# Flamingo gated layer: eight small transfers per quad issued from ScalarE's queue instead of SyncE's

## The reference, cut to what matters

```
x   (8, 512, 1024), ctx (8, 512, 1024), mask all ones, 16 heads of 32 channels
q = Wq @ layernorm(x) + bq ; k = Wk @ ctx + bk ; v = Wv @ ctx + bv     # per batch, channels first
dot  = q^T k / sqrt(32), masked ; p = softmax(dot, over keys)
x    = x + tanh(g_xattn) * (p v)
y    = fp8(layernorm(x) * scale) / scale ; w = fp8(W2 * scale1) / scale1
out  = x + tanh(g_ffn) * (y @ w)
```

## Time and profile before

| | us |
|---|---|
| median of the runs | 2694.86 (2690.07 to 2695.24) |
| the profiled execution's own time | 2675.94 |
| its span, first to last instruction | 2674.1 |
| PE busy | 2539.9 (95%) |
| DVE / POOL / ACT busy | 1990.7 / 1651.7 / 1425.5 |
| granted TensorE clock, mean | 0.977 |
| share of the chain that ended last: PE / DMA / `den_c<-den` of it | 62% / 6% / 5% |

### The profile page before, as it was taken

One profiled execution on the slowest core, in us unless ns is written; L12 is line 12 of the kernel. 1 busy time (PEld: TensorE's weight loads), 2 busy tenths in 40 slices (PEclk: granted clock), 3 DMA queues, 4 the chain that ended last, 5 costly groups with the idle time before them and its releaser, 6 DMA issues.

```text
span 2674.1 us, 41111 instructions
## 1 busy us (share of the span) xinstructions
PE 2539.9 (95%) x13425; PEld 1401.9 (52%) x13425; DVE 1990.7 (74%) x3251; ACT 1425.5 (53%) x2638; POOL 1651.7 (62%) x1265
## 2 busy tenths in 40 slices
PE   5999999969999999999999999999999999999995
PEld 4888888854444444444444444444444444444441
DVE  5766666738777888788777777887888888878763
ACT  2333333314565666565656556666666666656663
POOL 1433333314776777677766777777777777767674
PEclk8999999987999999999999999999999999999998
DMA  6666666553333344444333333333333444444301
GB/s 207 245 238 237 239 238 238 211 154 58 74 82 82 91 96 91 86 98 95 87 83 86 82 82 82 82 82 82 90 83 90 96 92 95 93 87 90 84 29 40
DMA packets 208250, 306.12 MB, mean 114 GB/s; under 512 B 41241, under 2 KB 108889, under 8 KB 208065
## 3 DMA queue, kind: packets, MB, share of 16 engines
q1 hardware_dynamic: 195920, 265.80, 39.6%
q10 hardware_dynamic: 12144, 38.02, 4.0%
HBM read 200.09 MB, written 102.11 MB: 113 GB/s over the span
## 4 chain that ended last, share of the span: by engine, by line
PE 62%; DMA 6%; DVE 5%; issue 3%; POOL 1%; ACT 1%; SPq 0%; DVEq 0%; ACTq 0%; POOLq 0%
PE s_bank L694 18%; PE o_bank L720 17%; PE x_bank L707 15%; PE d_bank L731 7%; DMA den_c<-den 5%; PE x_bank L755 4%; DVE part_max L872 4%; PE x_bank L746 1%; POOL pair_sum L965 1%; PE x_bank L738 1%; DMA q_st<-qx_scr 0%; ACT den L812 0%; DVE y L103 0%; POOL y L974 0%; ACT probs L800 0%
## 5 line engine op out<-in xcount | busy, mean ns | idle before, releaser
L965 POOL TENSOR_TENSOR pair_sum<-probs 128x512 f32<-128x512 f32 x1024 | 1283.4, 1285 | 544.6 <-ACT probs L800 544.6
L872 DVE TENSOR_REDUCE part_max<-x_bank 128x1 f32<-128x512 f32 x2048 | 1279.4, 682 | 375.2 <-PE x_bank L707 368.2
L800 ACT ACTIVATE probs<-s_bank 128x512 f32<-128x512 f32 x2048 | 1071.5, 604 | 656.4 <-PE s_bank L694 650.4
L694 PE MATMUL s_bank<-q_st,k_st 100*128 100x512 f32 x2048 | 876.1, 430 | 4.6 <-ACT probs L800 4.6
L707 PE MATMUL x_bank<-k_st,q_st 98*128 98x512 f32 x2048 | 826.7, 407 | 55.1 <-DVE part_max L872 32.8
L694 PEld LDWEIGHTS s_bank<-q_st,k_st 100*128 100x128 f32 x2048 | 387.0, 189 | 513.2 <-issue 265.7
L720 PE MATMUL o_bank<-probs,v_t 128*32 128x512 f32 x4096 | 551.3, 611 | 0.0
L707 PEld LDWEIGHTS x_bank<-k_st,q_st 98*128 98x128 f32 x2048 | 392.9, 192 | 182.8 <-DVE part_max L872 62.8
L731 PE MATMUL d_bank<-pair_sum,ones 128*32 128x512 f32 x2048 | 269.4, 598 | 2.7 <-POOL pair_sum L965 2.7
L322 POOL TENSOR_TENSOR stage_lo<-stage,stage_hi 128x512 fp32r<-128x512 f32 x128 | 186.5, 1480 | 120.8 <-ACT stage_hi L392 120.2
L392 ACT ACTIVATE stage_hi<-stage 128x512 fp32r<-128x512 f32 x128 | 79.8, 632 | 190.4 <-DVE stage L476 142.8
(11 more groups left out here) (99 smaller groups left out, 2102.4 us busy)
## 6 DMA issues: line engine op xcount, KB each, us to landing
k_st<-k_scr SPq DMA_DIRECT2D x96, 512.0 KB
q_st<-q_scr SPq DMA_DIRECT2D x192, 256.0 KB
c_raw<-in_ctx_dram ACTq DMA_DIRECT2D x32, 512.0 KB, 7.0
x_raw<-in_x_dram ACTq DMA_DIRECT2D x32, 512.0 KB, 6.2
k_scr<-stage_hi SPq DMA_DIRECT2D x64, 256.0 KB, 2.4
k_scr<-stage_lo SPq DMA_DIRECT2D x64, 256.0 KB, 2.6
v_scr<-stage SPq DMA_DIRECT2D x64, 256.0 KB, 2.7
q_scr<-stage_hi SPq DMA_DIRECT2D x64, 256.0 KB, 2.1
```

Of the source, the lines that this page charges most:

```text
L694: nc.tensor.matmul(s_bank_of(n, k)[:, :], k_st[p][0:KS, h, j * P:(j + 1) * P], q_st[p][0:KS, th, h, :], start=True, stop=True).then_inc(sc ...
L800: nc.scalar.activation(probs[:, c % PR, h, :], s_bank_of(n, k)[:, :], ACT.Exp).then_inc(exp_done, 1)
L872: nc.vector.tensor_reduce(part_max[:, th, sh, at:at + 1], x_bank_of("tile", k)[:, :], AX, ALU.max).then_inc(max_done, 2)
L965: nc.gpsimd.tensor_tensor(pair_sum[:, r % 2, h], probs[:, a, h], probs[:, a + 1, h], ALU.add).then_inc(pair_done, 1)
```

## The change

Eight transfers of a period change engine: `move_den`, `move_inv`, `spread_inv` and `set_max`, each for both halves of a quad, leave SP's stream and are written into ScalarE's, at fixed slots between the exponentials. On SP stay `stack`, `load_res`, `load_v`, `load_tm` and `store`. The semaphore `stacked`, which counted the loads of q and k over all quads, is split by the parity of the quad, because SP can now run ahead with the loads of the second quad. Sizes, data and conditions of the transfers are unchanged. The functions themselves move word for word, with `act` for `sp`.

```
-            stacked = [sem(f"stacked{i}", at) for i in range(TH)]
+            stacked = [[sem(f"stacked{i}{th}", at) for th in range(TH)] for i in range(2)]
...
-                            pe.wait_ge(stacked[th], 16 * STACK_DMAS[th] * (m + 1))
+                            pe.wait_ge(stacked[p][th], STACK_DMAS[th] * loads_of_parity(m, p))
...
+                    def move_den(m, th):
+                        act.wait_ge(den_copied, 2 * m + th + 1)
+                        act.dma_start(den_c[:, :], den[0:P:D, :]).then_inc(den_moved, 16)
...
+                            if k == 13 and real(n - 1):
+                                move_den(n - 1, 1)
+                            if k == 24 and real(n - 1):
+                                move_inv(n - 1, 1)
+                            if k == 24 and real(n):
+                                set_max(n, 1, p)
+                            if k == 29 and real(n - 1):
+                                spread_inv(n - 1, 1)
+                            if k == 45 and real(n):
+                                move_den(n, 0)
+                            if k == 57 and real(n):
+                                move_inv(n, 0)
+                            if k == 62 and real(n):
+                                spread_inv(n, 0)
...
+                            if k == 56 and real(n + 1):
+                                set_max(n + 1, 0, 1 - p)
...
-                        if real(n - 1):
-                            move_den(n - 1, 1)
-                            move_inv(n - 1, 1)
-                        if real(n):
-                            set_max(n, 1, p)
-                        if real(n - 1):
-                            spread_inv(n - 1, 1)
```

More of the change, by code:

```diff
@@ L825, in copy_y8, with move_inv, spread_inv, set_max @@
                                              x_bank_of("turn_y8", 27)[:, :].bitcast(BF16), ACT.Copy).then_inc(y8_copied, 1)
+                    def move_den(m, th):
+                        act.wait_ge(den_copied, 2 * m + th + 1)
+                        act.dma_start(den_c[:, :], den[0:P:D, :]).then_inc(den_moved, 16)
+                    def move_inv(m, th):
+                        act.wait_ge(inv_done, 2 * (2 * m + th + 1))
+                        act.dma_start(inv_scr[th].rearrange("h (u v) -> (h u) v", u=D), inv_c[:, :]).then_inc(inv_moved, 16)
+                    def spread_inv(m, th):
+                        act.wait_ge(inv_moved, 16 * (2 * m + th + 1))
+                        if counted(NORM_STEPS * (m - 1) + 1):
+                            act.wait_ge(norm_done, NORM_STEPS * (m - 1) + 1)
+                        act.dma_start(inv_b[:, th, :], inv_scr[th].unsqueeze(1).broadcast_to((QH, D, HALF))).then_inc(inv_spread, 16)
+                    def set_max(m, th, p):
+                        act.wait_ge(max_copied, 2 * m + th + 1)
+                        act.dma_start(q_st[p][KX:KS, th, :, :].bitcast(F32), max_rows[:, :].bitcast(F32)).then_inc(max_set, 16)
                     def scale_rstd(m):
@@ L1012, in stack @@
                         for at, part in ((0, 0), (D, 1), (2 * D, 0)):
-                            sp.dma_start(k_st[p][at:at + D, :, :].bitcast(F32), k_part[part]).then_inc(stacked[0], 16)
-                        sp.dma_start(k_st[p][96:KS, :, :].bitcast(F32), kx_q[:, bass.ds(m, 1), :].broadcast_to((4, QH, S))).then_inc(stacked[0], 16)
+                            sp.dma_start(k_st[p][at:at + D, :, :].bitcast(F32), k_part[part]).then_inc(stacked[p][0], 16)
+                        sp.dma_start(k_st[p][96:KS, :, :].bitcast(F32), kx_q[:, bass.ds(m, 1), :].broadcast_to((4, QH, S))).then_inc(stacked[p][0], 16)
                         for th in range(TH):
                             for at, part in ((0, 0), (D, 0), (2 * D, 1)):
-                                sp.dma_start(q_st[p][at:at + D, th, :, :].bitcast(F32), q_part[part][:, th]).then_inc(stacked[th], 16)
+                                sp.dma_start(q_st[p][at:at + D, th, :, :].bitcast(F32), q_part[part][:, th]).then_inc(stacked[p][th], 16)
                             row = qx_q[:, bass.ds(m, 1), th * HALF:(th + 1) * HALF]
-                            sp.dma_start(q_st[p][96:98, th, :, :].bitcast(F32), row.broadcast_to((2, QH, HALF))).then_inc(stacked[th], 16)
+                            sp.dma_start(q_st[p][96:98, th, :, :].bitcast(F32), row.broadcast_to((2, QH, HALF))).then_inc(stacked[p][th], 16)
                     def load_v(m, p):
@@ L1024, in load_v @@
                         sp.dma_start(v_t[p][:, :, :], v_scr[bass.ds(m, 1), :, :].rearrange("o (j s) d -> s (o j) d", s=P)).then_inc(v_loaded[p], 16)
[L1026 to L1040, removed]
                     def load_tm(m):
@@ L1069, in period @@
                             load_v(n + 1, 1 - p)
-                        if real(n - 1):
-                            move_den(n - 1, 1)
-                            move_inv(n - 1, 1)
-                        if real(n):
-                            set_max(n, 1, p)
-                        if real(n - 1):
-                            spread_inv(n - 1, 1)
                         if real(n):
                             load_tm(n)
-                        if real(n):
-                            move_den(n, 0)
                         if real(n - 2):
                             store(n - 2, p)
[L1083 to L1088, removed]
                     run(period)
```

3 lines of the change are left out of this document (removed).

## The result

The kernel after has a median of 2842.20 us (2842.01 to 2842.94, 4 runs) against 2693.74 of the kernel before beside it (2690.07 to 2695.24, 4 runs): ratio 1.0568, 95% interval 1.0539 to 1.0596. The forecast was 2650 and the range ended at 2696. The profiled execution has a span of 2840.3 us against 2674.1, and a mean granted clock of 0.945 against 0.977.

What follows compares the result with a forecast made beforehand. TensorE, 95% busy, was taken to stop mainly for the denominators' transfer queued behind loads; -39 + 3 + 1 = -35 us on 2675.94 gave 2641, or 2660 with a constant offset; forecast the middle, 2650, range 2632 to 2696.

Steps and rivals of the forecast that it cites:

- Part 4: SP's stream: its loads keep their start and contention, its remaining waits stand before `load_tm` and `store` alone; cost nothing.
- Part 3: Waits moved into ScalarE's stream: `spread_inv` issued later, landing just before `weigh` needs it; +1 us, bounds 0 and +9.
- Part 2: Cost to ScalarE of issuing eight transfers per period, delaying exponentials, chiefly in slot 13: +3 us, bounds 0 and +46.
- rival C: Slower: ScalarE's slot 13 issue takes 2.8 us each period, TensorE pays and its clock falls; 2725 us, chance 0.14.
- the price of 41 us: TensorE's stops for `den_c` and the half clock behind them, in the profiled execution; the most their removal can give.
- Part 1: `move_den` of th = 1 on ScalarE's queue passes the loads, landing 4.3 us after issue: -39 us.
- the bound of 11 us: What remains if all the short TensorE stops of 0.38 us stay, over 29 periods.
- residue of 2: Allowance, in us, for periods in which line 900 misses its boundary with GpSimd's pair sum by a little.
- Rival B: Denominators land as late as before, descriptors of both queues being handled behind the loads; 2697 us, chance 0.13.
- The +3: Us charged for ScalarE's `den_c` issue in slot 13 possibly being as slow as SP's there.
- the slack of 0.3 us: Margin expected between the landing of the spread inverse, near 1539.7, and GpSimd's `weigh` at 1540.00; 5.3 us before.
- the two readings of the 18.9 us: Runs' median above the profiled execution: constant offset, giving 2660 us, or more long stops, giving near 2641.

Runs made afterwards that it cites:

- e1: Kernel after, with `spread_inv` of th = 0 issued by SP again, ahead of the next loads: 2655.65 us, 0.9881 of the kernel before.
- e3: Kernel after, with each spread of the inverse cut into four transfers, one per head: 2657.51 us, 0.9888 of the kernel before.
- e4: Kernel after, with `spread_inv` of th = 0 moved from slot 62 to slot 25 of the next period: 2658.28 us, 0.9879 of the kernel before.
- e2: Kernel before, all transfers on SP, with the spread of th = 0 held until right before the loads: 2838.97 us, ratio 1.0563.
- e9: Kernel after, with 256 of the 512 columns in the spread of th = 0: 2694.66 us, 1.0039 of the kernel before.
- e10: Kernel after, with 64 of the 512 columns in the spread of th = 0: 2665.80 us, 0.9934 of the kernel before.
- e6: Kernel before, with SP issuing `move_den` of th = 1 ahead of `load_res` and `load_v`: 2629.63 us, ratio 0.9791.
- e5: Kernel before, with only `move_den` of th = 1 moved to ScalarE, in slot 13: 2647.53 us, ratio 0.9861.
- the probe: Extra 128 x 16 element transfer on ScalarE's queue in slot 6, added to the kernel after with the th = 0 spread in slot 25: 2655.16 us.
- e7: Kernel after with the th = 0 spread in slot 25, SP holding `load_res` and `load_v` until th = 1 denominators landed: 2631.18 us, 0.98 of the kernel before.

## Why the prediction was wrong, point by point

**Part 4, and the start of `spread_inv` in Part 3: the step that failed.** Part 4 said of SP's loads that "neither their start nor their contention changes". The start was right (they still begin with the last scores), the contention was not: it is the spread of half th = 0 that comes to meet them. Part 2 has the same gap: it took all slots but 13 to have no load in flight, from a stretch near slot 29, and slot 62 lies 0.4 us before the loads. Part 3 followed `spread_inv` of th = 1 from 1529.91 to slot 29 and never that of th = 0, from 4.3 us before the loads to 0.4 us before them. One transfer of 256 KB on four engines delays the loads by 5.8 us, since a load has landed only when its slowest engine has (the 17 late updates of 104). The margin of slot 19, which the prediction did not read, was 16.85 - 15.8 = 1.1 us. Cost: 142.9 us of stops and most of 57.2 us at a lower clock. e1, e3 and e4 take that away in three ways, e2 puts it into the kernel before, and e9 and e10 scale it. No rival had this mechanism; rival C, slower as well, named ScalarE's issue, which didn't slow.

**What bounds the kernel, and the price of 41 us: nearly right.** Removing the wait altogether is worth 46 us of the span (2674.1 to 2628.0 in e6), 52 between medians. The value is 5 to 11 above the ceiling I gave; a period of the kernel without any stop is 61.4 us, where I took 62.10 - 0.38 = 61.72.

**Part 1: its value nearly right by luck, its mechanism wrong.** The move alone (e5) brought 34 us, and -39 + 3 were forecast. But the estimate that each short packet waits for one load packet, and so a landing after 4.3 us, failed: 9.0 us in e5, 8.9 in e1, 9.2 in e4, 12.3 in the kernel after itself, 10.0 for the probe. A landing that still takes 10 us was the prediction's own sign of being wrong. By the medians the other queue wins only 0.7 to 1.0 us over the 9.9 of the kernel before; that is enough to tip the long stops into short ones, and the short ones stay, the bound of 11 us that Part 1 named and not its residue of 2. The rest of the gain, 18 us between e5 and e6 on one chip, needs the order: e6 and e7 issue the denominators before the last megabyte of loads. Rival B was the better description of the transfer and the poorer one of the time. The prediction counted 8 packets for each engine; the transfer runs on four, so it has 32. With that the same estimate would have given 32 x 0.3 + 1.9 = 11.5 us; but the probe, on 16 engines, took 10.0 as well, so the count of engines does not explain the landing either.

**Part 2: right.** ScalarE's issue of `den_c` over the whole program, against SP's in the earlier trace rows:

```profile
L829 ACTq DMA_DIRECT2D den_c<-den x64: 549/554/605, 669.2 to 2805.4; - x64
```

It never slows, though the DMA engines are as full then (share 1.08 from 1516 to 1520), so the slow issues of SP in the earlier trace rows belong to SP's queue and not to the full DMA engines. The +3 should have been 0.

**Part 3, the rest: within its bound.** `weigh` waits for the spread 13.9 us in all, 11.4 of them in the tail, where the kernel before waits 10.6. The other 2.5 us are nine short waits: the slack of 0.3 us was used up in nine periods. What they cost TensorE no run separates.

**The sum and the offset: not shown.** Which of the two readings of the 18.9 us is right no run decides; the kernel before had medians from 2681.7 to 2694.9 us in its groups of runs, so a part of it comes and goes with the group. Rival C's limit is 41/31 = 1.32 us in a period, not 1.35, which changes nothing here.

## What to carry to other kernels

When a group of small transfers is moved, write down for each of them, and each half of it, which bulk transfer it now overlaps, how many DMA engines it uses, and what margin the first consumer of that bulk transfer has; a transfer that is cut over few engines delays a load by about the time that one of those few needs for its share of the bytes. A second queue is not a fast lane: to make a short transfer land early beside bulk loads, issue it before them, or issue the bulk that nobody needs yet after it. Read the margins of transfers that never show up as waits, because these are the ones a change can turn into waits.

## What the runs showed of the hardware that was not expected

Where no load runs, the same 256 KB land in 4.8 us in one piece (th = 1, kernel before) and in 3.4 us in four pieces (e3), the issues of the four included. SP's issues get slow in the kernels with the whole late spread: `load_res` in the kernel after, over the program, against 355 ns (median) before:

```profile
L1071 SPq DMA_DIRECT2D res<-in_x_dram x32: 333/2231/3237, 692.3 to 2791.4; - x32
```

In e2 it is 2.1 us, in e4 and e9 0.35. ScalarE's issue 4 us later keeps to 0.55 us. That SP is held because four engines have no more room for its loads fits this, but is not shown. And the price of a stop grows faster than its length: by the distance of equal tiles, a period takes a median of 62.4 us in e10, 63.6 in e9 with 1.16 us of stop, and 68.4 in the kernel after with 4.76. The first stop costs its own length; from e9 to the kernel after 3.6 us more of stop cost 4.8, although the short stops for VectorE's maxima are gone there. From 700 to 2600 us the granted clock falls to 1.2 GHz 28 times in the kernel after, once in each period, and 4 times in e9.
